# Two graph-attention layers on one core: programs written out, first row factors spread by TensorE, layer 0 results in three pieces, head parts moved among the groups

## The chip, the core and the metric

The kernel runs on one core of one Trainium2 chip. The metric is the device time of one execution in microseconds (us). The engines are TensorE (PE, with its weight loads as PEld), VectorE (DVE), ScalarE (ACT), GpSimd (POOL) and SyncE (SP), each with a queue of instructions of its own that it works off in order; they wait for one another by semaphores.

## The reference

Eight graphs of 2048 nodes with 256 features, a dense adjacency matrix each, two attention layers with a residual:

```python
h = relu(layernorm(x));  x = x + gnn0(h, adj)      # one head
h = relu(layernorm(x));  x = x + gnn1(h, adj)      # four heads of 64 columns
# gnn: f = h W^T (+ b);  s_src, s_dst = f a_src, f a_dst
#      e[i, j] = leaky_relu(s_src[i] + s_dst[j], 0.2), masked where adj[i, j] == 0
#      out[i] = softmax_j(e[i, :]) f
```

A row without any edge gives the mean of f.

## The kernel before

**Factors instead of a softmax over pairs.** exp(leaky_relu(s + d)) is a product of a factor of the row and one of the column, with two different pairs of factors, for s + d above and below zero. Layer 0 makes tiles max(row factor, column factor) * mask (DVE, line 1214, `A` events) and multiplies them with the weighted features (PE, line 1006). Layer 1 compares row and column factors (ACT, line 782, or for a few groups DVE, line 1258), masks the bits for "negative" (DVE, line 1278, `N`) and "positive" (DVE, line 1282, `S`), and multiplies those bits as fp8 with features that are split into three bf16 parts (`Sw`) and two fp16 parts (`Sv`) (PE, lines 1022 and 1028, `G` events; a group is four column blocks of one head). The row factors of a chunk have to lie along the free axis on all 128 partitions, in `Rb`: five rows, one for layer 0 and four for the heads. Before, they are transposed (PE, line 944), moved (ACT, line 683), written to `R_dram` and read back with a broadcast (SP, lines 379 and 384).

**Chunks, batches, steps.** A graph (batch) has 4 chunks of 512 rows. Layer 1 runs five chunks behind layer 0 (`B_LAG`), so for each batch b = 1 to 7 there are these steps:

- the **first step** (`slot_f`): layer 0 of chunk 0 (16 `A` tiles on PE) beside the last features of layer 1 of batch b - 1: `T1` and `F1` are the transposes and products of a half chunk, `MV` moves a product out, `Y1` and `N1` are ACT's moves and normalisations for them. Then the maxima (`MX`, DVE `MAX` and `SHIFT`), exponentials (ACT `exps`), the mean (`MN`, `MEANL`), the rows (`RW`), and the parts of heads 0 and 1: `W` weighs them (DVE, line 1130), `first_part` rounds (ACT, line 697), `LF` takes off the first part (DVE, line 1135), `second_part` (ACT, line 701), `LS` gives the third (DVE, line 1140); POOL weighs and subtracts for `Sv` (lines 489 and 494), ACT rounds (lines 708, 713).
- **AB1**, **AB2**, **AB3**: layer 0 of chunks 1 to 3 beside layer 1 of the batch before; 16 `A` tiles and 16 `G` groups. AB1 also makes the parts of heads 2 and 3. After the last group of a head ACT moves the sums out (lines 809 to 812, `EB`) and POOL finishes the head (lines 553 to 574). After the last tile ACT moves the sums of layer 0 out (line 740, `EA`) and DVE adds them to x and takes the statistics for the next layernorm (`X1`: lines 1231 to 1246, then 1062 and 1066).
- the **last step** (`slot_g`): layer 1 of the last chunk beside the features of layer 0 of the next batch (`T`, `FE`).

**What sets the order.** The lists of events that `order`, `slot_f` and `slot_g` write by hand; each engine picks its own events out of them. `vector_order` puts an `A` tile between `N` and `S` where one stands ahead of a group. ACT compares up to `LEAD` groups ahead, into two slots (`CRING`); the tiles of layer 0 have four slots (`RING`). PE, DVE and ACT run batches 1 to 6 in a hardware loop (`looped`, line 314), batch 0 and batch 7 written out; SP and POOL are written out throughout.

## Time and profile before

| | |
|---|---|
| median of 3 runs | 2997.63 us (2993.99 to 3000.18) |
| the profiled execution | 2994.71 us, of it the span 2992.9 us |
| granted TensorE clock, mean | 0.952 of full |
| busy: PE, DVE, ACT, POOL | 85%, 66%, 55%, 46% of the span |

A row of the timeline gives start, duration, engine, line, operation, what it writes and reads, how many instructions are merged (x), and in brackets the idle time of the engine before it and what ended that. A fp32 product stands in the trace as two MATMUL rows' worth of count, so an `A` tile is x8. The table of stretches gives each engine's busy time, then the granted clock and the DMA share. The steps of a batch end where ACT moves the sums of layer 0 out (line 740): in the second batch at 649.9, 735.8, 811.8, 886.1 and (the next first step) 1011.5 us.

### The profile page before, as it was taken

How to read it: one execution, taken by the hardware profiler on the slowest of the kernel's cores; microseconds unless marked ns; L12 is line 12 of the kernel's file. 1: busy time of each engine (PE TensorE's matmuls, PEld its weight loads, DVE VectorE, ACT ScalarE, POOL GpSimd, SP SyncE). 2: the span in 40 equal slices, each digit the busy share in tenths (PEclk: the TensorE clock that was granted, in tenths of full speed). 3: DMA queues.
4: the chain of work that ended last, by engine and by line, in shares of the span. 5: the costliest groups of instructions: out<-in, count | busy, mean ns of one | idle time of the engine just before them, and what ended most of it. 6: DMA issues, size and time to landing. Idle time of an engine off the chain costs nothing.

```text
span 2992.9 us, 60549 instructions
## 1 busy us (share of the span) xinstructions
PE 2530.4 (85%) x22166; PEld 2261.4 (76%) x22166; DVE 1966.6 (66%) x3342; ACT 1660.0 (55%) x3170; POOL 1370.9 (46%) x1757
## 2 busy tenths in 40 slices
PE   4988799878998799987999879988799888996686
PEld 3876688867887588875888768887688867886676
DVE  1544666766666676657667576665666676668996
ACT  4124655645567465655556465664655655554664
POOL 2111445534455354443455434454444444446566
PEclk9998899989999899998999989999899999999899
DMA  7682244242442444422443324423244242211120
GB/s 131 70 96 38 36 75 72 45 80 40 71 74 51 68 62 74 72 48 48 75 76 62 57 41 75 75 54 65 36 74 76 52 75 35 62 36 36 37 54 19
DMA packets 332958, 181.38 MB, mean 61 GB/s; under 512 B 278240, under 2 KB 279392, under 8 KB 332640
## 3 DMA queue, kind: packets, MB, share of 16 engines
q1 hardware_dynamic: 314208, 143.64, 22.0%
q0 software_dynamic: 18432, 33.56, 13.0%
q8 instruction: 192, 3.15, 0.4%
q14 instruction: 126, 1.03, 0.1%
HBM read 193.60 MB, written 50.66 MB: 82 GB/s over the span
## 4 chain that ended last, share of the span: by engine, by line
PE 54%; DVE 19%; ACT 14%; issue 9%; POOL 3%; DMA 0%; DVEq 0%; ACTq 0%; SPq 0%; POOLq 0%
PE accA L1006 24%; PE accB L1022 12%; PE accB L1028 8%; ACT shared L782 8%; DVE shared L1258 4%; PE misc_ps L914 4%; DVE shared L1214 3%; DVE shared L1278 3%; PE accA L889 3%; ACT shared L621 2%; DVE xb L1239 1%; DVE xb L1246 1%; DVE stats L1062 1%; PE misc_ps L904 1%; PE accA L878 1%
## 5 line engine op out<-in xcount | busy, mean ns | idle before, releaser
L782 ACT ACTIVATE shared<-Rb,dd 128x512 int8<-128x512 f32 x1616 | 1017.7, 718 | 382.2 <-DVE shared L1278 381.9
L1006 PE MATMUL accA<-S,shared 128*128 128x257 f32 x4096 | 1009.3, 400 | 179.1 <-DVE shared L1214 162.2
L1022 PE MATMUL accB<-Sw,shared 128*128 128x195 bf16 x7680 | 978.5, 250 | 85.8 <-DVE shared L1282 56.5
L1006 PEld LDWEIGHTS accA<-S,shared 128*128 128x128 f32 x4096 | 794.7, 199 | 322.7 <-DVE shared L1214 195.9
L1028 PE MATMUL accB<-Sv,shared 128*128 128x130 f16 x7680 | 763.9, 223 | 0.0
L1022 PEld LDWEIGHTS accB<-Sw,shared 128*128 128x128 fp8e4 x7680 | 642.2, 99 | 142.3 <-issue 103.8
L1214 DVE SCALAR_TENSOR_TENSOR shared<-Rb,dd,mask 128x512 f32<-128x512 f32 x512 | 457.3, 909 | 268.1 <-PE accA L1006 213.9
L1028 PEld LDWEIGHTS accB<-Sv,shared 128*128 128x128 fp8e4 x7680 | 577.9, 99 | 0.9
L553 POOL TENSOR_SCALAR shared<-shared 128x260 f32<-128x260 f32 x128 | 136.9, 1070 | 761.8 <-ACT shared L812 719.7
L1278 DVE TENSOR_TENSOR shared<-shared,mask 128x512 uint32<-128x512 uint32 x512 | 402.1, 785 | 125.6 <-ACT shared L782 118.6
L1282 DVE TENSOR_TENSOR shared<-shared,mask 128x512 uint32<-128x512 uint32 x512 | 413.5, 808 | 12.0
L1258 DVE TENSOR_SCALAR shared<-Rb,dd 128x512 uint8<-128x512 f32 x432 | 245.3, 631 | 13.0 <-PE accB L1028 13.0
L809 ACT ACTIVATE shared<-accB 128x390 f32<-128x390 f32 x120 | 58.7, 489 | 319.2 <-PE accB L1028 283.8
L1079 DVE TENSOR_TENSOR S<-misc_ps,bias 128x264 f32<-128x264 f32 x128 | 54.7, 427 | 223.1 <-PE misc_ps L914 222.7
L914 PE MATMUL misc_ps<-WT,yT 128*128 128x264 f32 x512 | 147.5, 412 | 55.4 <-ACT yT L650 54.2
L494 POOL TENSOR_TENSOR S<-S,Sv 128x1040 f32<-128x1040 f32 x32 | 70.5, 2203 | 199.3 <-ACT Sv L708 199.3
L567 POOL TENSOR_TENSOR denB<-denB,minus_one 128x4 f32<-128x4 f32 x128 | 149.7, 1169 | 23.5 <-POOL denB L565 23.5
L914 PEld LDWEIGHTS misc_ps<-WT,yT 128*128 128x128 f32 x512 | 93.4, 199 | 72.6 <-ACT yT L650 58.7
L889 PE MATMUL accA<-WT,shared 128*128 128x258 f32 x512 | 125.8, 393 | 21.2 <-ACT S L658 21.2
L740 ACT ACTIVATE shared<-accA 128x1028 f32<-128x1028 f32 x32 | 32.9, 1027 | 189.8 <-PE accA L1006 189.8
L474 POOL TENSOR_SCALAR var_eps<-mv 128x4 f32<-128x4 f32 x64 | 23.8, 372 | 228.3 <-DVE mv L1066 226.2
L889 PEld LDWEIGHTS accA<-WT,shared 128*128 128x128 f32 x512 | 95.0, 194 | 41.9 <-ACT S L658 29.6
(106 smaller groups left out, 2566.1 us busy)
## 6 DMA issues: line engine op xcount, KB each, us to landing
Rb<-R_dram SPq DMA_DIRECT2D x160, 256.0 KB, 3.6
adj_bytes<-in_adj POOLq DMA_DIRECT2D x128, 256.0 KB, 5.3
xb<-in_x SPq DMA_DIRECT2D x32, 512.0 KB, 5.0
out<-xb SPq DMA_DIRECT2D x32, 512.0 KB, 3.6
mask<-adj_bytes SPq DMA_TRANSPOSE x256, 4.1
shared<-in_W SPq DMA_DIRECT2D x2, 256.0 KB, 3.1
R_dram<-R_rows SPq DMA_DIRECT2D x8, 32.0 KB, 1.8
shared<-in_a SPq DMA_DIRECT2D x8, 0.2 KB, 10.6
```

The lines of the kernel that those rows point to most:

```text
L553: pool.tensor_scalar(low, low, 1 / LOW, None, ALU.mult)
L567: pool.tensor_tensor(denB[:, :], denB[:, :], minus_one[:, :], ALU.pow)\
L782: last = nc.scalar.activation(cmp[:, slot, jj // 2, of_pair(jj % 2, 0, CI)], Rb[:, h, :], ACT.Sign, bias=w[1][:, JG * g + jj, h:h + 1], sc ...
L889: last = nc.tensor.matmul(accA[:, 2 + k % 2, 0:E0], yT[:, t % 2, kc, k * P:(k + 1) * P], WT[0][:, kc, :], start=kc == 0, stop=kc == KC - 1)
L914: last = nc.tensor.matmul(misc_ps[:, 0:E1], yT1[:, kc, k * P:(k + 1) * P], WT[1][:, kc, :], start=kc == 0, stop=kc == KC - 1)
L1006: last = nc.tensor.matmul(accA[:, k, 0:F + 1], tiles[:, j % RING, k * P:(k + 1) * P], S0[:, j, 0:F + 1], start=j == 0, stop=j == NJ - 1)
L1022: nc.tensor.matmul(acc[:, bank, col:col + NS], bits[:, g % BRING, 1, jj // 2, of_pair(jj % 2, k * P, P)], Sw[:, j, h, :, :].rearrange("p a ...
L1028: last = nc.tensor.matmul(acc[:, bank, col:col + NN], bits[:, g % BRING, 0, jj // 2, of_pair(jj % 2, k * P, P)], Sv[:, j, h, :, :].rearran ...
L1214: nc.vector.scalar_tensor_tensor(out=tiles[:, j % RING, :], in0=Rb[:, H, :], scalar=w[0][:, j, :], in1=mask[:, n % 2, j // 2, of_pair(j % ...
L1258: last = nc.vector.tensor_scalar(bits_u8[:, g % BRING, 0, jj // 2, of_pair(jj % 2, 0, CI)], Rb[:, h, :], w[1][:, JG * g + jj, h:h + 1], 25 ...
L1278: nc.vector.tensor_tensor(n_bits, src.bitcast(u32), chunk_mask, ALU.bitwise_and)\
L1282: nc.vector.tensor_tensor(s_bits, n_bits, chunk_mask, ALU.bitwise_xor)\
```

## The change

Four things, all in the order of work and in how the first chunk's rows come about; the arithmetic of the outputs is unchanged.

1. PE, DVE and ACT have no hardware loop any more: all eight batches are written out.
2. For chunk 0 the row factors no longer go through DRAM: `spread_rows` on PE (event `SP`) transposes each factor column, broadcast to 128 columns, into PSUM (4 transposes for layer 0, 16 for layer 1, into `accB` and `misc_ps`), and `move_first_rb` on ACT copies them to `Rb` (1 or 4 copies of 128x512). SP loads `Rb` only for chunks 1 to 3. `turn_rows` waits until the copies are made.
3. `X1` is cut into `X1` (sum of the mean), `X2` (sum of layer 0), `X3` (statistics), which stand among the first groups of the next step; the last half product of a chunk is moved out there too (`("MV", 7)`), and `T1`, `F1` stand later in the steps.
4. In AB1 the first group stands ahead of the first tiles, two groups are compared at the start, and the parts of heads 2 and 3 are spread over the first four groups. In the first step all four `F1` and one `T1` stand between the tiles, and `MX`, `MN`, `RW` two or three tiles later.

```diff
-    def order(do_a, do_b, do_l, stats=None, x1_before=False, parts=False, feats=False):
+
+    def order(do_a, do_b, do_l, stats=None, first=False, feats=False, results=(), late_move=False):
         events = []
+        x1, x2, x3 = [[(x, 1)] * bool(results) for x in ("X1", "X2", "X3")]
         for h in range(H):
             last = h == H - 1
             a = [[("A", G * h + i)] * do_a for i in range(G)]
             g = [[("G", h, i)] * do_b for i in range(G)]
             load = [("L", 2, h)] * do_l
-            early = [("X1", 1)] * (x1_before and h == (0 if do_b else 1))
             st = [("ST", stats)] * (stats is not None and h == (2 if do_b else H - 1))
             eb = [("EB", h)] * do_b
             if last:
-                events += a[0] + [("MV", 1)] * feats + a[1] + a[2] + a[3] + [("EA",)] * do_a + g[0] + [("F1", 3)] * feats
-                events += g[1] + [("MV", 2)] * feats + load + g[2] + g[3] + st * (not do_b)
-                events += [("X1", 0)] * (do_a and do_b) + [("MV", 3)] * feats + eb
-            elif h == 0 and parts:
-                events += a[0] + a[1] + [("NM", 2), ("W", 2), ("HI", 2)] + g[0] + [("LF", 2), ("MID", 2), ("HIGH", 2)]
-                events += g[1] + [("NR", 2), ("LS", 2)] + a[2] + [("NM", 3), ("W", 3), ("HI", 3)] + load + g[2]
-                events += [("LF", 3), ("MID", 3), ("HIGH", 3), ("LOW", 2)] + a[3]
-                events += g[3] + [("NR", 3), ("LS", 3)] + early + eb + [("LOW", 3)]
+                events += a[0] + [("MV", 1)] * feats + a[1] + [("F1", 2)] * feats + a[2] + a[3] + [("EA",)] * do_a
+                events += g[0] + g[1] + load + g[2] + [("MV", 2), ("F1", 3)] * feats + g[3] + st * (not do_b)
+                events += [("X1", 0)] * ("end" in results) + [("MV", 3)] * (feats and not do_b) + eb
+            elif h == 0 and first:
+                events += g[0] + a[0] + a[1] + [("NM", 2), ("W", 2), ("HI", 2)] + g[1] + [("LF", 2), ("MID", 2), ("HIGH", 2)]
+                events += a[2] + [("NR", 2), ("LS", 2), ("NM", 3), ("W", 3), ("HI", 3)] + load + g[2] + [("LOW", 2)]
+                events += a[3] + [("LF", 3), ("MID", 3), ("HIGH", 3)] + x1 + g[3] + [("NR", 3), ("LS", 3)] + eb
+                events += [("LOW", 3)]
+            elif h == 0:
+                events += a[0] + a[1] + [("MV", 7)] * late_move + g[0] + x1 + g[1] + x2 + a[2] + load + g[2] + x3
+                events += a[3] + g[3] + eb
             else:
                 on1, on2 = feats and h == 1, feats and h == 2
-                events += early * (not do_b) + [("N1", 0)] * on1 + a[0] + a[1] + g[0] + [("F1", 1)] * on2 + g[1]
-                events += [("T1", 0), ("Y1", 0), ("N1", 1)] * on1 + [("MV", 0)] * on2 + a[2] + load + g[2]
-                events += [("F1", 0)] * on1 + [("T1", 1), ("Y1", 1)] * on2 + a[3] + st + g[3] + [("F1", 2)] * on2
-                events += early * do_b + eb
+                t0 = [("T1", 0), ("Y1", 0), ("N1", 1)] * on1
+                f0 = [("F1", 0)] * on1
+                late = x2 * (first and h == 1), x3 * (first and h == 1)
+                events += [("N1", 0)] * (on1 and not first) + a[0] + late[0] + a[1] + g[0] + late[1] + [("F1", 1)] * on2
+                events += [("N1", 0)] * (on1 and first) + g[1] + (not first) * t0 + [("MV", 0)] * on2
+                events += a[2] + load + g[2] + (first * t0 or f0) + a[3] + st
+                events += [("T1", 1), ("Y1", 1)] * on2 + g[3] + first * f0 + eb
...
-    STEP_AB = [None] + [order(1, 1, 1, stats=1, x1_before=c == 1, parts=c == 1, feats=True) for c in range(1, NC)]
-    STEP_AB_LAST = [None] + [order(1, 1, c < NC - 2, x1_before=c == 1, parts=c == 1, feats=True)
-                             for c in range(1, NC)]
+    STEP_AB, STEP_AB_LAST = [[None] + [order(1, 1, more or c < NC - 2, stats=1 if more else None, first=c == 1, feats=True,
+                                             results=["before"] + ["end"] * (c == NC - 1), late_move=c > 1)
+                                       for c in range(1, NC)] for more in (True, False)]
...
-        def looped(eng, prog):
-            start(prog)
-            with eng.Fori(1, B - 1) as b:
                 batch(prog, b, True)
             end(prog)
...
             def features(b, L=0):
                 store_rows(b, L)
-                for u in [H] if L == 0 else range(H):
-                    load_rb(b, 0, u)
...
+            def move_first_rb(b, L):
+
+                act.wait_ge(S["misc_done"], 4 * layer_index(b, L) + 3)
+                for u in [H] if L == 0 else range(H):
+                    src = misc_ps[:, :] if u >= H - 1 else accB[:, u, :]
+                    nc.scalar.activation(Rb[:, u, :], src, ACT.Copy).then_inc(S[f"rb_made{L}"], 1)
...
             def slot_f(b, beside):
+                move_half(b - 1, NC - 1, 0)
+                norm_half(b - 1, NC - 1, 1)
+                if beside:
+                    scale_features(2)
                 move_half(b - 1, NC - 1, 1)
                 if beside:
-                    for t in range(2, NC):
-                        scale_features(t)
+                    scale_features(3)
                 exps(b - 1, 1)
+                move_first_rb(b - 1, 1)
                 first_part(b - 1, 0)
                 move_rows(b - 1, 1)
...
-                ahead, nxt = {}, mine[0] + 1
+                ahead, nxt = {}, mine[1 if kind == "AB1" else 0] + 1
                 for e in events:
                     if e[0] == "G":
                         i = G * e[1] + e[2]
-                        upto = min(i + (LEAD - 1 if i < G else LEAD), HG - 1)
+                        upto = min(i + (LEAD if i >= G else LEAD - 2 if kind == "AB1" else LEAD - 1), HG - 1)
...
-            looped(act, Program(features, lambda: None, step, slot_f, slot_g))
+            written_out(Program(features, lambda: None, step, slot_f, slot_g))
...
-            def turn_rows(b, L):
+            def spread_rows(b, L):
                 i = layer_index(b, L)
                 pe.wait_ge(S["exp_ready"], 2 * i + 2)
                 pe.wait_ge(S["misc_used"], 3 * i + 2)
+                if L == 1:
+                    pe.wait_ge(S["b_moved"], H * NC * b + 1)
+                for u in [H] if L == 0 else range(H):
+                    dst = misc_ps if u >= H - 1 else accB[:, u, :]
+                    for k in range(CH):
+                        last = nc.tensor.transpose(dst[:, k * P:(k + 1) * P], R[:, u, k:k + 1].to_broadcast([P, P]),
+                                                   ident[:, :])
+                last.then_inc(S["misc_done"], 1)
+
+            def turn_rows(b, L):
+                i = layer_index(b, L)
+                pe.wait_ge(S[f"rb_made{L}"], (b + 1) * (1 if L == 0 else H))
...
-                events = [("A", 0), ("F1", 2), ("A", 1), ("F1", 3), ("A", 2), ("A", 3), ("MX",), ("A", 4), ("A", 5), ("MN",),
-                          ("A", 6), ("RW",)] + [("A", j) for j in range(7, NJ)]
+                events = [("F1", 0), ("A", 0), ("F1", 1), ("A", 1), ("T1", 1), ("A", 2), ("F1", 2), ("A", 3), ("F1", 3),
+                          ("A", 4), ("A", 5), ("MX",), ("A", 6), ("A", 7), ("MN",), ("A", 8), ("SP",), ("A", 9),
+                          ("RW",)] + [("A", j) for j in range(10, NJ)]
...
-                          ("G", 2, 1), ("FE", 3), ("G", 2, 2), ("MX",), ("G", 2, 3), ("MN",), ("G", 3, 0), ("RW",),
-                          ("G", 3, 1), ("T1", 0), ("G", 3, 2), ("F1", 0), ("G", 3, 3), ("F1", 1), ("T1", 1)]
+                          ("G", 2, 1), ("FE", 3), ("G", 2, 2), ("MX",), ("G", 2, 3), ("MN",), ("G", 3, 0), ("SP",),
+                          ("G", 3, 1), ("RW",), ("G", 3, 2), ("T1", 0), ("G", 3, 3)]
...
-                events = [("A", 0), ("A", 1), ("A", 2), ("MV", 2), ("A", 3), ("MV", 3), ("MAX",), ("A", 4), ("A", 5),
-                          ("SHIFT",), ("W", 0), ("A", 6), ("MEANL",), ("A", 7), ("LF", 0), ("A", 8), ("A", 9), ("LS", 0), ("A", 10),
-                          ("W", 1), ("A", 11), ("A", 12), ("LF", 1), ("A", 13), ("LS", 1), ("A", 14), ("A", 15)]
+                events = [("A", 0), ("A", 1), ("MV", 0), ("A", 2), ("MV", 1), ("A", 3), ("MV", 2), ("A", 4), ("MV", 3), ("MAX",),
+                          ("A", 5), ("A", 6), ("SHIFT",), ("W", 0), ("A", 7), ("MEANL",), ("A", 8), ("LF", 0), ("A", 9),
+                          ("A", 10), ("LS", 0), ("W", 1), ("A", 11), ("A", 12), ("LF", 1), ("A", 13), ("A", 14), ("LS", 1),
+                          ("A", 15)]
...
+                    events += {("G", 0, 0): [("X2", 1), ("MV", 7)], ("G", 0, 1): [("X3", 1)]}.get(e, [])
...
                         last.then_inc(S["a_sum"], 1)
+                        continue
+                    if e[0] == "X2":
+                        n1 = n - e[1]
+                        xs = xb[:, n1 % XSLOTS, :, :]
                         dve.wait_ge(S["a_rec"], n1 + 1)
...
                         last.then_inc(S["x1_ready"], 1)
+                        continue
+                    if e[0] == "X3":
+                        n1 = n - e[1]
                         dve.wait_ge(S["x1_ready"], n1 + 2)
```

Where the instructions moved, as they stand in the built programs. First DVE in the middle of the first step (batch 7 of before, batch 1 of the change; all four rows with `Rb` are tiles of layer 0, `split` and `Sw` are the head parts), before:

```order
L1106 TENSOR_SCALAR ss<-ss 128x64
L1110 MEMSET S 128x64
L1130 TENSOR_TENSOR split<-S,wv 128x1040
L1214 SCALAR_TENSOR_TENSOR shared<-Rb,dd,mask 128x512
L1119 SCALAR_TENSOR_TENSOR mean_h<-misc_ps,bias 128x264
L1214 SCALAR_TENSOR_TENSOR shared<-Rb,dd,mask 128x512
L1135 TENSOR_TENSOR split<-split,Sw 128x1040
L1214 SCALAR_TENSOR_TENSOR shared<-Rb,dd,mask 128x512 x2
L1140 TENSOR_TENSOR Sw<-split,Sw 128x16x65
```

and of the change:

```order
L1139 TENSOR_SCALAR ss<-ss 128x64
L1143 MEMSET S 128x64
L1163 TENSOR_TENSOR split<-S,wv 128x1040
L1249 SCALAR_TENSOR_TENSOR shared<-Rb,dd,mask 128x512
L1152 SCALAR_TENSOR_TENSOR mean_h<-misc_ps,bias 128x264
L1249 SCALAR_TENSOR_TENSOR shared<-Rb,dd,mask 128x512
L1168 TENSOR_TENSOR split<-split,Sw 128x1040
L1249 SCALAR_TENSOR_TENSOR shared<-Rb,dd,mask 128x512 x2
L1173 TENSOR_TENSOR Sw<-split,Sw 128x16x65
```

The sequence is the same, but it stands one tile later in the step: the single tiles are `A` 6 and 7 before, and `A` 7 and 8 now.

Then ACT at the same place, before:

```order
L672 ACTIVATE R<-ss 128x16x4
L676 ACTIVATE dd<-dd 128x64
L697 ACTIVATE Sw<-split 128x16x65
L683 ACTIVATE R_rows<-misc_ps 128x128
L701 ACTIVATE Sw<-split 128x16x65
```

and of the change:

```order
L678 ACTIVATE R<-ss 128x16x4
L682 ACTIVATE dd<-dd 128x64
L690 ACTIVATE Rb<-accB 128x512 x3
L690 ACTIVATE Rb<-misc_ps 128x512
L710 ACTIVATE Sw<-split 128x16x65
L696 ACTIVATE R_rows<-misc_ps 128x128
L714 ACTIVATE Sw<-split 128x16x65
```

The copies of the spread rows stand between the exponentials and the first rounding of head 0.

Last DVE from the end of AB1 into AB2 (before: batch 7):

```order
L1282 TENSOR_TENSOR shared<-shared,mask 128x512
L1231 TENSOR_SCALAR alone_now<-shared 128x4
L1232 TENSOR_SCALAR alone<-shared 128x4
L1233 TENSOR_SCALAR denA<-shared 128x4
L1236 RECIPROCAL denA<-denA 128x4
L1239 SCALAR_TENSOR_TENSOR xb<-mean_h,alone_now,xb 128x256 x4
L1246 SCALAR_TENSOR_TENSOR xb<-shared,denA,xb 128x256 x4
L1062 BN_STATS stats<-xb 128x6 x4
L1066 BN_AGGR mv<-stats 128x2 x4
L1079 TENSOR_TENSOR S<-misc_ps,bias 128x264
L1214 SCALAR_TENSOR_TENSOR shared<-Rb,dd,mask 128x512 x2
L1258 TENSOR_SCALAR shared<-Rb,dd 128x512 x4
```

and of the change:

```order
L1324 TENSOR_TENSOR shared<-shared,mask 128x512
L1249 SCALAR_TENSOR_TENSOR shared<-Rb,dd,mask 128x512 x2
L1112 TENSOR_TENSOR S<-misc_ps,bias 128x264
L1300 TENSOR_SCALAR shared<-Rb,dd 128x512 x4
L1320 TENSOR_TENSOR shared<-shared,mask 128x512
L1324 TENSOR_TENSOR shared<-shared,mask 128x512
L1266 TENSOR_SCALAR alone_now<-shared 128x4
L1267 TENSOR_SCALAR alone<-shared 128x4
L1268 TENSOR_SCALAR denA<-shared 128x4
L1271 RECIPROCAL denA<-denA 128x4
L1274 SCALAR_TENSOR_TENSOR xb<-mean_h,alone_now,xb 128x256 x4
L1300 TENSOR_SCALAR shared<-Rb,dd 128x512 x4
```

The result of the chunk moved from ahead of the first group's comparison to behind it; line 1079 (now 1112) is the move of the last half product.

## Rows read from the trace of the kernel before

**Rows 1.** The page, parts 1 and 4: busy time by engine; the chain that ended last.
```profile
PE 2530.4 (85%) x22166; PEld 2261.4 (76%) x22166; DVE 1966.6 (66%) x3342; ACT 1660.0 (55%) x3170; POOL 1370.9 (46%) x1757
...
PE 54%; DVE 19%; ACT 14%; issue 9%; POOL 3%; DMA 0%; DVEq 0%; ACTq 0%; SPq 0%; POOLq 0%
```

**Rows 2.** Stretches: AB1, AB2, AB3, last plus first step looped, the same written out.
```profile
649.90:735.80 85.90, 65.79 (x535) 58.06 (x536) 55.92 (x88) 55.68 (x94) 34.41 (x41) 0.90 0.23 38
735.80:811.80 76.00, 71.23 (x667) 65.68 (x666) 50.66 (x92) 44.51 (x82) 37.09 (x53) 0.98 0.44 74
811.80:886.10 74.30, 69.44 (x666) 64.06 (x664) 50.75 (x92) 44.43 (x81) 37.15 (x53) 1.00 0.43 72
886.10:1011.50 125.40, 108.06 (x908) 93.56 (x905) 83.57 (x140) 65.67 (x146) 61.52 (x74) 0.96 0.36 67
2333.50:2451.30 117.80, 105.27 (x907) 92.02 (x904) 83.67 (x140) 65.65 (x146) 62.00 (x74) 0.99 0.38 65
```

**Rows 3.** Timeline at the loop's edge, second to third batch: all engines.
```profile
968.08 2.88 DVE L1214 SCALAR_TENSOR_TENSOR shared<-Rb,dd,mask 128x512 f32<-128x512 f32 x3 [3.15 <-issue]
...
969.01 1.07 PE L1006 MATMUL accA<-S,shared 128*128 128x257 f32 x2 [3.29 <-DVE shared L1214]
```

**Rows 4.** Timeline at the same place of batch 7, written out: PE.
```profile
2413.14 2.00 PE L1006 MATMUL accA<-S,shared 128*128 128x257 f32 x8
```

**Rows 5.** Timeline of a first step from the maxima on: PE, DVE, ACT.
```profile
620.58 0.60 PE L926 MATMUL misc_ps<-ident,d_part 128*128 128x128 f32 x4
...
623.38 1.24 DVE L1130 TENSOR_TENSOR split<-S,wv 128x1040 f32<-128x1040 f32 x1 [0.64 <-ACT dd L676]
...
624.54 0.78 DVE L1214 SCALAR_TENSOR_TENSOR shared<-Rb,dd,mask 128x512 f32<-128x512 f32 x1
624.66 1.09 ACT L697 ACTIVATE Sw<-split 128x1040 bf16<-128x1040 f32 x1 [1.31 <-DVE split L1130]
...
625.58 0.43 DVE L1119 SCALAR_TENSOR_TENSOR mean_h<-misc_ps,bias 128x264 f32<-128x264 f32 x1 [0.26 <-PE misc_ps L936]
...
627.62 1.23 DVE L1135 TENSOR_TENSOR split<-split,Sw 128x1040 f32<-128x1040 f32 x1
```

**Rows 6.** Timeline: nearest rows to a spread and to its copies.
```profile
240.77 1.09 PE L904 MATMUL misc_ps<-ident,y 128*128 128x128 f32 x4 [3.65 <-ACT y L639]
...
730.74 0.60 ACT L812 ACTIVATE shared<-accB 128x520 f32<-128x520 f32 x1
```

**Rows 7.** Timeline of the end of a first step and of AB1.
```profile
649.92 1.03 ACT L740 ACTIVATE shared<-accA 128x1028 f32<-128x1028 f32 x1 [5.04 <-PE accA L1006]
...
651.23 3.73 PE L1006 MATMUL accA<-S,shared 128*128 128x257 f32 x16 [1.43 <-ACT shared L740]
...
654.24 0.69 DVE L1282 TENSOR_TENSOR shared<-shared,mask 128x512 uint32<-128x512 uint32 x1
...
663.83 2.19 POOL L494 TENSOR_TENSOR S<-S,Sv 128x1040 f32<-128x1040 f32 x1 [10.34 <-ACT Sv L708]
663.87 2.69 DVE L1214 SCALAR_TENSOR_TENSOR shared<-Rb,dd,mask 128x512 f32<-128x512 f32 x1
...
666.62 3.80 PE L1006 MATMUL accA<-S,shared 128*128 128x257 f32 x8 [5.68 <-DVE shared L1214]
...
687.27 2.94 PE L1006 MATMUL accA<-S,shared 128*128 128x257 f32 x6 [8.54 <-DVE shared L1214]
```

**Rows 8.** Timeline of AB1's last move and of AB2's opening.
```profile
727.69 1.16 PE L914 MATMUL misc_ps<-WT,yT 128*128 128x264 f32 x4 [2.48 <-ACT yT L650]
...
736.88 0.17 DVE L1231 TENSOR_SCALAR alone_now<-shared 128x4 f32<-128x4 f32 x1 [4.91 <-ACT shared L740]
...
737.52 2.49 DVE L1239 SCALAR_TENSOR_TENSOR xb<-mean_h,alone_now,xb 128x256 f32 x4
...
748.58 3.33 DVE L1258 TENSOR_SCALAR shared<-Rb,dd 128x512 uint8<-128x512 f32 x4
...
753.92 0.62 PE L1022 MATMUL accB<-Sw,shared 128*128 128x195 bf16 x4 [2.29 <-DVE shared L1282]
```

More of the change, by code:

```diff
@@ L523, in slot_g @@
                 at = STEP_B.index(("EB", 1))
[L524 removed]
+                step("G", [("X3", 1)] + STEP_B[:at] + [("ST", 1)] * more + STEP_B[at:], b, NC)
             def step(kind, events, b, c):
@@ L796, in step @@
                     compare(mine[0])
+                if kind == "AB1":
+                    compare(mine[1])
                 for e in events:
```

65 lines of the change are left out of this document (34 added, 31 removed), and 4 rows, old and new, of the table events.

## The prediction, made before the changed kernel ran

> **What bounds the kernel now.** I read the page first: TensorE is busy 85% of the span and holds 54% of the chain that ended last, VectorE 19% of it [rows 1]. That makes every idle stretch of PE the thing to look for. The table of stretches then shows where they are [rows 2]: AB2 and AB3 have 71.2 and 69.4 us of PE work in 76.0 and 74.3 us and are bound by PE. AB1 has less work (65.8) and takes 85.9 us, and its granted clock is 0.90, so TensorE also ran there at 1.2 instead of 2.4 GHz for a fifth of the time. Last and first step together take 125.4 us in the loop, but 117.8 us for the same work in batch 7, which is written out. The timeline says what PE waits for: DVE, whose queue is in order and is itself held by ACT and POOL.
>
> From these rows two prices that I use below: a tile of layer 0 costs PE 3.73 / 2 = 1.87 us [rows 7], and a group 2.3 us (AB2's 71.2 less 16 tiles, four half products of 1.16 [rows 8] and two transposes of half tiles, over 16).
>
> **The change, part by part.** Sums are per batch, and stand against the profiled execution's own 2994.7 us; the median of the runs shown is 2.9 us above that, so I add to 2997.6.
>
> *Loops written out.* At the loop's edge DVE starts 3.15 us late without any wait for another engine, and PE's first tile comes after 3.29 us of idle time [rows 3]; in batch 7 the first tile has no idle time before it and its x8 take 2.00 us [rows 4]. The whole difference is 125.4 - 117.8 = 7.6 us, and there are five such edges (the last one leaves the loop and is the 117.8 itself): **-38 us**.
>
> *The first step.* This is where I expect to lose. Its parts, against the written-out 117.8:
> - Its first instruction on PE is now the half product `F1` 0, which waits for ACT's move `Y1` 0. That stands on ACT behind the move of the last head's sums (three operations, the longest 0.60, [rows 6]), which waits for the last group. So PE idles about 2.7 us where it idled 0.6 before: +2.1, and +1.0 for the slower clock after it.
> - The spread for layer 0: 4 transposes, +0.6. For layer 1: 16 transposes. I take 4 x 0.5 = 2.0 us at 2.4 GHz, from the x4 that took 0.60 with its latency [rows 5]. The row at 1.2 GHz has 1.09 for four [rows 6], so 4.4 us is the other end.
> - `MX` moved behind tile 5, but DVE still has only one tile made ahead of it. From the end of `MX` (621.18) to the end of the tile behind the weighing `W` 0 (625.32) are 4.1 us [rows 5], and PE now has one tile (1.87) to cover them, where it had two: +2.3. The next tile stands directly behind the mean, which PE makes just ahead of it: 0.43 + 0.78 less 0.3 of today: +1.0.
> - The largest: on ACT the four copies of the spread rows stand ahead of the first rounding (line 697, now 710), they wait for the spread, the spread stands on PE behind tile 8, and DVE takes tile 9 only after `LF` 0, which waits for that rounding. So tile 8, spread, copies, rounding, `LF` 0 and tile 9 are one chain. Four copies of 512 columns at 0.5 each (0.60 for 520 columns [rows 6], less the 0.1 by which one overlaps the next), 1.09, 1.23 and 0.78 [rows 5] make 5.1 us in which PE has nothing. +5.1.
> - `RW` now follows tile 9 and ACT's second rounding waits for it, as do `LS` 0, `W` 1 and tile 11; with the slower clock after 5 us of idle time: +2.0.
>
> Together **+16 us** for each of batches 2 to 7. For batch 1 the half products that are spread among tiles now stood alone ahead of the tiles before, with waits like the 3.65 us at 240.77 [rows 6], so only +8. In all +104. Bounds: +6 a batch if DVE finds its rounding ready (only real work and the opening are left), +20 if the spread runs at 1.2 GHz.
> The trip through DRAM that is removed hid behind other work here: no comparison waits for a row transfer of chunk 0. It was bare only at the start of the program (-4), and at its end the copies lengthen the chain to the first group (+2.5).
>
> *AB1.* Before, PE idles 1.43, 5.68 and 8.54 us [rows 7] and three times under 1.1: 17.6 us in all until the second group of head 1. The 5.68 is a tile behind `LS` 2, which waits for ACT; the 8.54 is tile 4 behind the whole result `X1`. Both orders are mended. But the first group is now first on PE, and its bits need the move of the sums, a comparison, `N` and `S`: from 649.92 to 654.93 [rows 7], so PE idles 5.3 us there instead of 1.43. I followed DVE's new queue with the durations of rows 5 and 7. Four POOL operations of 2.2 us fall into this step, and each holds a DVE operation that meets it until it ends (a tile took 2.69 instead of 0.78 beside one, [rows 5, 7]). Then the third group's bits come 2.2 us late, the fourth's 3.3, tile 5 0.8, the second group of head 1 1.7: with the opening 13.3 us. That is -4.3. The late move `Y1` 1 ahead of `F1` 2 (2.48 us, [rows 8]) goes, since a group and two tiles now cover it: -2.5. Fewer waits raise the clock from 0.90, tile rows of 3.80 against 2.00 us being its price [rows 4, 7]: -2.2. **-9 a batch**, -63 in all; between -4 (more operations held) and -15 (none).
>
> *AB2 and AB3.* They too lose the 2.48: -2.5 each. But their opening gets worse. The second group waits for bits that DVE compares itself, 2.29 us now [rows 8]. In the change, DVE's queue there begins with the move of the last half product, which comes at the same distance from the last group. From it to the second group's bits, two tiles (1.5) leave and the result's first part enters (four small ones of about 0.17, then 2.49): +1.7. The tile behind it waits for `X2` on top, about 1.3, where the clock was full before. So -0.8 for AB2, +0.5 for AB3: **-2 us** for seven batches. Bounds for the two together: -5 to +6 a batch, since a comparison of four rows took 3.33 us [rows 8] beside POOL's work and may take half of that without it.
>
> *The last step* gets 0.4 us longer (a transpose behind the second group waits for ACT's later normalisation): +3.
>
> Sum: -38 + 104 - 4 + 2.5 - 63 - 2 + 3 = +2.5, so **3000 us**.
>
> **The rivals.**
> 1. *Faster.* The held operations of DVE fall into its own waits. In AB1 DVE waits for ACT twice in this stretch, and if three of the four 1.9 us fall there, AB1 gains 6 more: -42, 2958. For it speaks that DVE is busy for only 56 of AB1's 86 us [rows 2]; against it that today three of four do hit an operation that PE waits for.
> 2. *Slower.* The result's pieces make DVE the bound at 14 openings. `X1`, `X2` and `X3` are 8 us of DVE work that stood where DVE waited 4.91 us for the sums [rows 8], and now stand where PE has no bits in store. If POOL's last head slows them as it slowed 2.49 and 3.33, each opening costs 3 us more: +42, 3042. It decides from the point at which DVE's work between the last half product and the second group's bits exceeds what PE has to do there, a group, two tiles and a group (8.3 us). Against it: 1.7 and 1.3 of it are counted above.
> 3. *Slower.* The spread of layer 1 runs at 1.2 GHz and leaves the clock there for the tile behind it: four transposes took 1.09 us in such a stretch [rows 6] against 0.60 [rows 5], so 4.4 us instead of 2.0, and a tile 3.80 [rows 7] against 2.00 [rows 4]: +4 a batch, +28, 3028. The row at 0.60 stood in a stretch of full clock and speaks against it; the idle time ahead of tile 7 speaks for it. The Trainium skill ("TensorE: Matmul & The Clock Gate", "Part 4: PE-mode transpose") has the full clock not engaging for transposes, which do not count as PE-busy in the same way; that is this rival. No stretch of before has so many transposes in a row, so no row here decides it.
> 4. *The change doesn't do what it says.* Written-out code may have to be fetched while it runs, and the 7.6 us may come back as pauses spread over the batch: 3038. Batch 7 speaks against it. The Trainium skill ("Runtime: NRT & Kernel Launch", "Instruction fetch mechanics") does too: sequential code is fetched ahead, and a taken branch outside the window stalls; the 3.15 us of rows 3 agree, and by it the sum stays.
>
> **How the numbers follow.** A measurement of this kernel can tell 0.2% (6 us) from no change. My own case, gains and losses cancel: 0.36, alone 2980 to 3020 (of it faster 0.08, same 0.17, slower 0.11). Rival 1: 0.32, faster. Rival 2: 0.18, rival 3: 0.08, rival 4: 0.06, slower. That is 0.40 faster, 0.17 same, 0.43 slower. The range takes in the bounds of AB1 and the first step as far as 8 in 10: 2955 to 3045.
>
> **What would show it.** Right: no pause without a releaser on DVE between batches; in every first step PE idle about 5 us ahead of tile 9, released by a DVE tile, and DVE idle for ACT's line 710; AB1 near 77 us; last plus first step near 134 us; AB2 and AB3 near 75. Wrong: last plus first step under 125 us (then the chain through the copies is not bare, and I am too high by up to 60), AB1 over 82, or AB2 and AB3 over 78 (rival 2).

## The result, and the profile of the changed kernel

The changed kernel takes 3040.6 us (median; 3039.6 to 3046.0), the kernel before 2996.0 beside it: a ratio of 1.015, with a 95% interval of 1.013 to 1.017. It is slower by 45 us, where I forecast 3000. The profiled execution has a span of 3038.2 us against 2992.9 before.

Parts 1 and 4 of the changed kernel's page, which answer to [rows 1]:

```profile
PE 2563.2 (84%) x22326; PEld 2305.3 (76%) x22326; DVE 1951.3 (64%) x3342; ACT 1686.2 (55%) x3210; POOL 1395.4 (46%) x1757
...
PE 58%; DVE 17%; ACT 14%; issue 7%; POOL 4%; SPq 0%; DMA 0%; POOLq 0%; ACTq 0%; DVEq 0%
```

Read alone, they tell almost nothing: PE has 160 matmuls more and nearly the same share of the span. The stretches say more. This is the table by stretch of batch 3, to be held against [rows 2]: AB1, AB2, AB3, last plus first step (from one evacuation of layer 0's sums to the next; then PE, PEld, DVE, ACT and POOL busy, the granted clock, the DMA share and GB/s).

```profile
1030.10:1112.40 82.30, 66.54 (x535) 59.60 (x535) 60.11 (x91) 56.23 (x94) 33.07 (x38) 0.90 0.27 47
1112.40:1186.40 74.00, 71.01 (x666) 65.61 (x665) 50.45 (x93) 44.59 (x81) 39.13 (x53) 0.98 0.42 76
1186.40:1260.20 73.80, 69.65 (x667) 64.29 (x666) 49.15 (x91) 44.62 (x82) 38.05 (x53) 1.00 0.41 73
1260.20:1395.40 135.20, 109.64 (x927) 96.63 (x924) 78.95 (x138) 68.14 (x151) 63.29 (x77) 0.96 0.28 47
```

AB1 went from 85.9 to 82.3 us (I expected 77), AB2 from 76.0 to 74.0 and AB3 from 74.3 to 73.8 (expected 75), last plus first step from 125.4 to 135.2 (expected 134). The other batches repeat the four within 0.2 us, but for batch 1: 81.2 for AB1, 74.1 for AB3, and 137.1 for its last step with the next first step. Batch 1's own first step grew from 84.4 to 98.5, the part behind the last evacuation from 303.6 to 317.1.

The pause of DVE without a releaser at the loop's edge, 3.15 us in [rows 3], is gone. In its place DVE now waits for an engine, the half product `F1` 0:

```profile
967.49 1.40 DVE L1249 SCALAR_TENSOR_TENSOR shared<-Rb,dd,mask 128x512 f32<-128x512 f32 x2
976.50 0.43 DVE L1112 TENSOR_TENSOR S<-misc_ps,bias 128x264 f32<-128x264 f32 x1 [7.61 <-PE misc_ps L934]
```

In the timeline the first step looks as forecast. Changed kernel, first step of batch 3, PE; rows with a wait and the spread between them:

```profile
975.30 1.16 PE L934 MATMUL misc_ps<-WT,yT 128*128 128x264 f32 x4 [2.20 <-ACT yT L656]
...
994.78 3.13 PE L1039 MATMUL accA<-S,shared 128*128 128x257 f32 x8 [2.54 <-DVE shared L1249]
...
1000.54 2.00 PE L1039 MATMUL accA<-S,shared 128*128 128x257 f32 x8 [1.19 <-DVE shared L1249]
1002.38 1.47 PE L969 MATMUL accB<-ident,R 128*128 128x128 f32 x12
1003.69 0.60 PE L969 MATMUL misc_ps<-ident,R 128*128 128x128 f32 x4
1009.42 3.54 PE L1039 MATMUL accA<-S,shared 128*128 128x257 f32 x8 [5.13 <-DVE shared L1249]
...
1019.51 4.69 PE L1039 MATMUL accA<-S,shared 128*128 128x257 f32 x13 [4.71 <-DVE shared L1249]
```

These are the waits of `F1` 0, of tile 7, of the tile behind the mean, of tile 9, and one that I had not priced by itself, 4.71 us at tile 11. ScalarE and VectorE show why tile 9 is late. ACT first, then DVE:

```profile
1004.39 1.58 ACT L690 ACTIVATE Rb<-accB 128x512 f32<-128x512 f32 x3 [11.71 <-PE misc_ps L969]
1005.84 0.62 ACT L690 ACTIVATE Rb<-misc_ps 128x512 f32<-128x512 f32 x1
1006.31 1.11 ACT L710 ACTIVATE Sw<-split 128x1040 bf16<-128x1040 f32 x1
...
1007.46 1.24 DVE L1168 TENSOR_TENSOR split<-split,Sw 128x1040 f32<-128x1040 f32 x1 [6.97 <-ACT Sw L710]
1008.62 1.41 DVE L1249 SCALAR_TENSOR_TENSOR shared<-Rb,dd,mask 128x512 f32<-128x512 f32 x2
```

The rounding (line 710) needs only 1.1 us, but DVE has been idle for it for 6.97 us: it stands behind four copies, which wait for the spread.

What I had not seen is in AB1. Its openings are there (5.26, 3.01, 1.36, 0.36, 1.47 us; I had worked out 13.3 together, they are 11.5), and then comes a wait that my list lacks. Changed kernel, AB1 of batch 3, POOL, DVE, ACT and PE:

```profile
1064.43 0.87 POOL L559 TENSOR_SCALAR shared<-shared 128x260 f32<-128x260 f32 x1 [7.59 <-DVE xb L1257]
...
1065.69 0.38 DVE L1099 BATCH_NORM_AGGREGATE mv<-stats 128x2 f32<-128x6 f32 x4
...
1073.41 0.91 POOL L580 TENSOR_TENSOR xb<-xb,shared 128x256 f32<-128x256 f32 x1 [0.18 <-POOL shared L576]
1074.41 0.56 POOL L480 TENSOR_SCALAR var_eps<-mv 128x4 f32<-128x4 f32 x1
...
1077.12 0.20 POOL L487 TENSOR_TENSOR shift<-rstd,neg_mean 128x4 f32<-128x4 f32 x1
...
1077.43 1.09 ACT L645 ACTIVATE y<-xb,shift,rstd 128x256 f32<-128x256 f32 x2 [5.72 <-issue]
...
1078.67 1.09 PE L924 MATMUL misc_ps<-ident,y 128*128 128x128 f32 x4 [4.31 <-ACT y L645]
1079.55 3.63 PE L1039 MATMUL accA<-S,shared 128*128 128x257 f32 x8
```

PE waits for `T1` 0, that for ACT's normalisation `N1` 0 (line 645), that for POOL's `shift` (line 487). DVE has the statistics ready at 1066.07 (line 1099), but POOL works on head 0's sums (lines 559 to 580, the event `EB` 0) until 1074.3, since `X3` comes behind `EB` 0 in its queue. The profile calls the wait of ACT "issue" and names no engine; the releaser had to be found by following what the instruction reads.

### The profile page after: what moved, and what is told of

It reads as the page before. It is cut to its first block, busy times and chain, and to the rows that moved or that the text cites. A ratio compares the mean times of both kernels' runs of the same rounds, so it can differ in the third digit from the quotient of the medians.

```text
span 3038.2 us, 57409 instructions
## 1 busy us (share of the span) xinstructions
PE 2563.2 (84%) x22326; PEld 2305.3 (76%) x22326; DVE 1951.3 (64%) x3342; ACT 1686.2 (55%) x3210; POOL 1395.4 (46%) x1757
## 4 chain that ended last, share of the span: by engine, by line
PE 58%; DVE 17%; ACT 14%; issue 7%; POOL 4%; SPq 0%; DMA 0%; POOLq 0%; ACTq 0%; DVEq 0%
PE accA L1039 25%; PE accB L1055 13%; PE accB L1061 9%; ACT shared L798 6%; PE misc_ps L934 4%; DVE shared L1300 4%; PE accA L909 3%; DVE shared L1320 2%; ACT shared L627 2%; DVE xb L1274 2%; DVE shared L1249 1%; DVE shared L1324 1%; DVE split L1163 1%; PE misc_ps L924 1%; DVE xb L1285 1%
## 5 line engine op out<-in xcount | busy, mean ns | idle before, releaser
L1055 PE MATMUL accB<-Sw,shared 128*128 128x195 bf16 x7680 | 993.2, 253 | 159.0 <-DVE shared L1324 95.5
L1055 PEld LDWEIGHTS accB<-Sw,shared 128*128 128x128 fp8e4 x7680 | 651.1, 100 | 213.1 <-issue 177.6
L1061 PE MATMUL accB<-Sv,shared 128*128 128x130 f16 x7680 | 775.2, 225 | 0.0
L1061 PEld LDWEIGHTS accB<-Sv,shared 128*128 128x128 fp8e4 x7680 | 588.2, 100 | 2.1
L1249 DVE SCALAR_TENSOR_TENSOR shared<-Rb,dd,mask 128x512 f32<-128x512 f32 x512 | 426.0, 846 | 203.6 <-PE accA L1039 200.6
L1320 DVE TENSOR_TENSOR shared<-shared,mask 128x512 uint32<-128x512 uint32 x512 | 395.9, 773 | 138.8 <-ACT shared L798 128.7
L1324 DVE TENSOR_TENSOR shared<-shared,mask 128x512 uint32<-128x512 uint32 x512 | 442.1, 863 | 12.2
L1300 DVE TENSOR_SCALAR shared<-Rb,dd 128x512 uint8<-128x512 f32 x432 | 227.0, 589 | 14.2 <-PE accB L1061 14.2
L934 PEld LDWEIGHTS misc_ps<-WT,yT 128*128 128x128 f32 x512 | 94.0, 195 | 33.6 <-ACT yT L656 19.3
L569 POOL TENSOR_TENSOR shared<-shared 128x260 f32<-128x260 f32 x128 | 101.1, 790 | 23.5 <-POOL shared L566 23.5
L495 POOL TENSOR_TENSOR S<-S,v 128x1040 f32<-128x1040 f32 x32 | 68.9, 2153 | 92.9 <-DVE split L1163 88.5
```

Of the source, the lines that this page charges most:

```text
L934: last = nc.tensor.matmul(misc_ps[:, 0:E1], yT1[:, kc, k * P:(k + 1) * P], WT[1][:, kc, :], start=kc == 0, stop=kc == KC - 1)
L1055: nc.tensor.matmul(acc[:, bank, col:col + NS], bits[:, g % BRING, 1, jj // 2, of_pair(jj % 2, k * P, P)], Sw[:, j, h, :, :].rearrange("p a ...
L1061: last = nc.tensor.matmul(acc[:, bank, col:col + NN], bits[:, g % BRING, 0, jj // 2, of_pair(jj % 2, k * P, P)], Sv[:, j, h, :, :].rearran ...
L1249: nc.vector.scalar_tensor_tensor(out=tiles[:, j % RING, :], in0=Rb[:, H, :], scalar=w[0][:, j, :], in1=mask[:, n % 2, j // 2, of_pair(j % ...
L1300: last = nc.vector.tensor_scalar(bits_u8[:, g % BRING, 0, jj // 2, of_pair(jj % 2, 0, CI)], Rb[:, h, :], w[1][:, JG * g + jj, h:h + 1], 25 ...
L1320: nc.vector.tensor_tensor(n_bits, src.bitcast(u32), chunk_mask, ALU.bitwise_and)\
```

## Experiments

Ten kernels. Times are medians, each beside the kernel before, which had 2990 to 2994 in these runs. Run names are those of the headings.

### e1_loops_out: the loops alone

```diff
-            looped(pe, Program(features, lambda: None, step, slot_f, slot_g))
+            written_out(Program(features, lambda: None, step, slot_f, slot_g))
```
(in the kernel before; the same for `act` and `dve`)

> The kernel before with the loops of TensorE, VectorE and ScalarE written out, nothing else. My theory (the term 'loops written out', -38): the five edges of 7.6 us go, so about 2958 us (2950 to 2966), with all six stretches of last and first step at 117 to 119 us instead of five at 125.4, and no pause of VectorE without a releaser between batches. Rival (the written-out code is fetched while it runs, rival 4): the edges' time comes back as pauses without a releaser elsewhere; 2990 us or more.

Measured: 2956.5 us against 2993.6, ratio 0.988 (0.986 to 0.989), so -37.1. The six stretches of last and first step take 115.8 to 117.9 us, where [rows 2]'s written-out line has 117.8 and the looped one 125.4:

```profile
1229.30:1346.60 117.30, 104.82 (x907) 92.10 (x904) 81.68 (x138) 65.62 (x145) 62.65 (x74) 0.99 0.36 67
```

The term of -38 stands, and rival 4 is out. By the stretches the five edges gave 42 us and the first batch's, which I had not counted, 3 more (84.4 to 81.3); AB1 to AB3 and the ends took some 7 of them back. Most of that is AB3, 75.7 us instead of 74.3 at a granted clock of 0.98 instead of 1.00. The waits without a releaser ahead of DVE's tiles (line 1214) went from 19.3 us in five waits to 0.2 us, and ACT's ahead of line 650, 11.5 us in five, are gone.

### e3_norm_first: POOL's order in AB1

The changed kernel, in POOL's step:

```diff
+                if kind == "AB1":
+                    events = [e for e in events if e != ("X3", 1)]
+                    at = events.index(("EB", 0))
+                    events = events[:at] + [("X3", 1)] + events[at:]
```

> The changed kernel (3040.6 us), but in the first combined step GpSimd does the normalization that ScalarE's first move-over waits for ahead of the eight operations on head 0's sums, and no longer behind them. Theory: the idle of TensorE of 4.28 us ahead of the first transposition (line 924) of this step hangs on these eight operations; moved, it falls to under 1 us, that step falls from 82.3 to about 78.5, and the time by seven of these, to about 3012 us (3008 to 3020). Rival: head 0's sums come 3 us later and the wait turns up behind them (ScalarE's copies of the sums of head 1, then TensorE at head 2's first group): the step stays within 1 us of 82.3 and the time at 3035 or more. Second rival: another late work (transposed tiles, a comparison) stands right behind; about half of the gain, 3025.

Measured: 2992.6 us, ratio to the kernel before 0.9999 (0.999 to 1.001). Four small operations, moved past ten others (I had counted eight) on an engine that is busy for 33 of 82 us, give -48 (-45 by the ratios), about as much as the changed kernel loses in all. AB1 is 75.1 in every batch. POOL and ACT in AB1 now:

```profile
1052.16 0.47 POOL L480 TENSOR_SCALAR var_eps<-mv 128x4 f32<-128x4 f32 x1 [9.43 <-DVE mv L1103]
...
1054.85 0.34 POOL L487 TENSOR_TENSOR shift<-rstd,neg_mean 128x4 f32<-128x4 f32 x1
1055.16 0.87 POOL L563 TENSOR_SCALAR shared<-shared 128x260 f32<-128x260 f32 x1
...
1057.49 1.08 ACT L649 ACTIVATE y<-xb,shift,rstd 128x256 f32<-128x256 f32 x2
...
1064.02 0.69 POOL L584 TENSOR_TENSOR xb<-xb,shared 128x256 f32<-128x256 f32 x1 [0.18 <-POOL shared L580]
```

The gain is 7.1 a batch where the idle was 4.3, so my 28 us were low by 20. Most of the rest is the clock, and the stretch shows it:

```profile
1016.00:1091.20 75.20, 64.06 (x536) 57.69 (x536) 60.05 (x91) 55.95 (x95) 33.14 (x38) 0.93 0.32 51
```

PE does the same matmuls in 64.06 us and no longer in 66.54, at 0.93 instead of 0.90. In the changed kernel PE starts again behind the wait at 0.50 (the lower level, 1.2 GHz), as the rows in the last section show. Both rivals fall: head 0's sums come 4.5 us later in the step and nobody waits for them.

### e4_steps_only and e5_steps_norm: the steps' new order without the new first step

e4: the kernel before, written out, with the change's `order`, its result in three pieces, the comparisons further ahead and the B steps' order; first step, the last step's tail and all rows through DRAM as before. e5 is e4 with the four lines of e3_norm_first. The pieces that differ from the changed kernel, in TensorE's program:

```diff
-                events = [("F1", 0), ("A", 0), ("F1", 1), ("A", 1), ("T1", 1), ("A", 2), ("F1", 2), ("A", 3), ("F1", 3),
-                          ("A", 4), ("A", 5), ("MX",), ("A", 6), ("A", 7), ("MN",), ("A", 8), ("SP",), ("A", 9),
-                          ("RW",)] + [("A", j) for j in range(10, NJ)]
+                events = [("A", 0), ("F1", 2), ("A", 1), ("F1", 3), ("A", 2), ("A", 3), ("MX",), ("A", 4), ("A", 5), ("MN",),
+                          ("A", 6), ("RW",)] + [("A", j) for j in range(7, NJ)]
```

> The kernel before, written out, with the new order of the steps AB1, AB2, AB3 and of the matching parts of the B steps (layer 0's results in three pieces, the parts of heads 2 and 3 among the groups, comparisons further ahead), but the first step of a batch, the tail of the last one and the rows through DRAM as before. Theory: AB1 82.3 and AB2, AB3 74.0 and 73.7 as in the changed kernel, last and first step at 118: 2958 less 27 less 18 is 2913, and some 8 us more in the end part from the first B step: 2915 to 2925. Rival: what AB1 and the others gain in the changed kernel is only work handed to the first step (the F1 0, F1 1, T1 1 moves), so the last and first step grow by as much here: 2945 to 2960.

> As the run before it (new order of AB1 to AB3 and B, first step and rows of before), with GpSimd's normalization ahead of the operations on head 0's sums in AB1. Theory: AB1 near 78.5, so 4 us a batch less, 2885 to 2897. Rival (the wait turns up behind head 0's sums, which come 3 us later): no difference to the run before it, within 5 us.

Measured: e4 2910.6 us, ratio 0.972 (0.970 to 0.974); e5 **2865.9 us**, ratio 0.957 (0.956 to 0.959). e4 against e1 is -45.9, so the new order of the steps is a gain of its own and no loan from the first step: last plus first step stays at 118.1 to 119.4. e5 against e4 is -44.7: the same wait, worth the same as in the changed kernel. Both came out under my ranges. For e4 I had put 8 us on the end part, which grew by 1.2. For e5 I had again priced the wait at its length alone, and it is 19 us under the range. e5 beats both kernels, by 4.3% and 5.7%. Its stretches, AB1 and last plus first step:

```profile
971.40:1046.50 75.10, 61.88 (x535) 55.72 (x536) 59.97 (x91) 55.90 (x94) 33.03 (x38) 0.98 0.32 49
...
1194.70:1312.70 118.00, 104.83 (x907) 91.99 (x904) 80.68 (x138) 65.72 (x145) 62.92 (x77) 0.99 0.37 67
```

AB1 has the same length as in e3 although its clock is 0.98 instead of 0.93 and PE is busy for 2.2 us less: once the wait is gone, AB1 waits for DVE's bits, and what a faster PE saves in work it idles at its five openings, 13.1 us in e5 and 11.0 in e3.

### e2_part_first: the rounding ahead of the copies

The changed kernel, ScalarE, first step:

```diff
-                move_first_rb(b - 1, 1)
                 first_part(b - 1, 0)
+                move_first_rb(b - 1, 1)
```

> The changed kernel (3040.6 us) with one swap in ScalarE's program of the first step: head 0's first part (line 710) goes ahead of the four copies of the spread rows, and no longer behind them. Theory (the chain tile 8, spread, four copies, rounding, LF 0, tile 9 of my prediction costs 5.1 us a batch): TensorE's 5.12 us ahead of tile 9 nearly go, seven times, and the time falls by 30 to 40 us, to about 3005; the last and first step goes from 135.2 to about 130. Rival: the second rounding (line 714) still stands behind the rows' copy, and VectorE's LS 0 and tile 11 take the time back: under 10 us saved, 3030 or more.

Measured: 3010.0 us, ratio 1.006 (1.005 to 1.008), so 31 us less than the changed kernel (26 by the ratios to the kernel before). Last plus first step is 130.2 to 132.9. PE in the first step of the next batch:

```profile
1352.51 2.00 PE L1039 MATMUL accA<-S,shared 128*128 128x257 f32 x8 [1.18 <-DVE shared L1249]
1358.41 0.33 PE L976 MATMUL misc_ps<-ident,R 128*128 128x128 f32 x1 [0.42 <-ACT Rb L690]
...
1365.19 10.16 PE L1039 MATMUL accA<-S,shared 128*128 128x257 f32 x38 [4.72 <-DVE shared L1249]
```

The 5.13 at tile 9 is gone and the 4.7 at tile 11 stayed: the chain through the copies is real, and its idle time has the size that I gave it. The stretch got only 2.3 to 5.0 us shorter, because the clock takes part of the gain back. Where it is 132.9 the waits are the same as in these rows, but tile 7 and tiles 11 to 15 ran partly at 0.50: 3.42 and 11.50 us instead of 2.00 and 10.59 (all 40 rows).

### e6_rows_dram and e9_rows0_spread: layer 1's rows back through DRAM

e6 is the changed kernel with these edits (and the counts of `misc_done` that go with them); e9 is e6 with the four lines of e3_norm_first.

```diff
             def features(b, L=0):
                 store_rows(b, L)
+                for u in range(H) if L == 1 else []:
+                    load_rb(b, 0, u)
...
-                move_first_rb(b - 1, 1)
...
-                        spread_rows(fb, fl)
+                        if fl == 0:
+                            spread_rows(fb, fl)
```

> The changed kernel with layer 1's first chunk of rows through DRAM as before (no spread and no ScalarE copies in the first step, layer 0's spread kept), everything else as changed. Theory (spread, copies and the waits behind them are 9.7 us a batch of the first step by my terms 0.6 + 2.0 + 5.1 + 2.0): last and first step from 135.2 to about 125.5, first B work no later, and the time about 60 to 70 us lower, near 2975. Rival 1: the moved order (F1, maxima and rounding two tiles later) is what costs, and the spread lies in its shadow: 3020 or more. Rival 2: the trip through DRAM then arrives late for AB1, whose compares come earlier now: AB1 grows by over 2 us a batch.

> The changed kernel with GpSimd's normalization first in AB1 (as e3_norm_first) and layer 1's rows through DRAM (as e6_rows_dram): what is left of the change against e8_order_only (2918.3 us) is the spread of layer 0's row alone. Theory: e6_rows_dram less the 45 to 48 us of the normalization, 2935 to 2938, so layer 0's spread, ScalarE's copy and the rows' copy behind it cost about 18 us or 3 to 4 us a batch in the last step (129.5 against 125.5). Rival: the two undoings share their gain (the same low clock), and the time is 2950 or more.

Measured: e6 2982.6 us, ratio 0.9975 (0.9965 to 0.9986), 58 us under the changed kernel (53 by the ratios); e9 2939.5 us, ratio 0.982 (0.981 to 0.984). Last plus first step is 129.3 to 129.7 in e6 (127.4 once), where I expected 125.5, so I had the spread 4 us a batch too dear there: it takes 5.7 us of it, and 9.1 in the first batch's first step. AB1 did not grow, so the trip through DRAM arrives in time. e9 is 1.5 us over my range. It lies 43 under e6 and 53 under e3, and its last plus first step at 128.8 stands 3.3 above e8's, which follows.

### e7_spread_only, e8_order_only, e10_spread_swap: one half at a time, on e5

e7 is e5 with layer 1's rows spread, in the first step's order of before (`("A", 6), ("SP",), ("A", 7), ("RW",)`); e8 is e5 with the change's order of the first step and of the last one's tail, rows through DRAM; e10 is e7 with the swap of e2_part_first.

> The kernel of the run e5_steps_norm (2865.9 us) with layer 1's first chunk of rows spread by TensorE and copied by ScalarE, in the first step's order of before. Theory: as the undoing of it, 9 to 10 us a batch, 2926 to 2936, with last and first step at 127 to 128. Rival: with tiles, maxima and rounding in the order of before the chain has two tiles of slack and the spread costs only its own 2.6 us: 2880 to 2890.

> The kernel of the run e5_steps_norm (2865.9 us) with the changed kernel's order of the first step and of the last one's tail (F1 0, F1 1, T1 1 and VectorE's moves in the first step, maxima and mean two tiles later), rows through DRAM. Theory: F1 0's wait 2.1, the wait ahead of tile 7 of 2.3, ahead of the tile behind the mean 1.0, and the clock, 6 to 8 us a batch: 2910 to 2925. Rival: the order costs as much as the whole of last and first step's 17 us and the spread nothing: 2980 or more. Third possibility: the order alone is worth nothing either way (2866), and it costs only together with the spread.

> The kernel of e7_spread_only (2912.2 us; layer 1's row spread, order of before) with head 0's first part ahead of the four copies. Theory: of the 46 us that the spread costs there, TensorE's idle of 2.58 us ahead of tile 8 hangs on the copies in ScalarE's queue (7 x 2.6 = 18), and the rest is the spread's own time on TensorE: 2890 to 2897, still above e5_steps_norm (2865.9). Rival: the copies are needed as early by the rows' transposition, whose wait then shows instead: 2905 or more.

Measured: e7 2912.2 (ratio 0.974, 0.972 to 0.975), e8 2918.3 (0.975, 0.974 to 0.977), e10 2889.8 (0.966, 0.964 to 0.968). So on e5 the order alone costs 52, the spread alone 46. e7 lies between my theory and the rival: its row on PE in the first step is

```profile
1316.88 1.35 PE L1055 MATMUL accA<-S,shared 128*128 128x257 f32 x5 [2.58 <-DVE shared L1264]
```

2.58 us bare instead of 5.13. From the end of the spread (1311.75) to this tile it is 5.13 us here too, but the spread stands behind tile 6, and tile 7 (1.90 us) is made ahead of `LF` 0 and lies ready behind it. e10 takes these away and is 22 us faster, as expected; 24 us remain over e5: the 16 transposes (1.9 us, seven times, and 3.7 once at the end) and what is left of the waits. In neither order of ScalarE does the spread pay for a DMA round trip that nobody waited for.

In e8 the wait at tile 11 shows alone. e5 has none there; its longest one behind `RW` stands ahead of tile 14. PE of e8, then of e5, and DVE of e8:

```profile
1326.18 4.22 PE L1018 MATMUL accA<-S,shared 128*128 128x257 f32 x9 [4.71 <-DVE shared L1225]
```
```profile
1308.97 3.30 PE L1019 MATMUL accA<-S,shared 128*128 128x257 f32 x14 [2.32 <-DVE shared L1228]
```
```profile
1322.31 3.11 DVE L1142 TENSOR_TENSOR split<-S,wv 128x1040 f32<-128x1040 f32 x1
```

`LS` 0 and `W` 1 now stand back to back ahead of tile 11 on DVE, and `W` 1 took 3.11 us there beside POOL's work, against 1.24 alone [rows 5]. In e5 a tile stands between the two and takes the hold (2.67 us), and PE's waits behind `RW` are four, 3.6 us together. So this place gives only 1.1 of the 7.4 us by which the order lengthens the stretch. 3.7 come from the waits of tiles 7 and 8, 2.54 and 1.18 us, which e5 does not have; 1.2 are more busy time of PE at 0.96 of the clock instead of 0.99, and most of the rest is the wait of `F1` 0, 2.19 us.

### The ladder

Each line differs from the one above it in one thing.

| kernel | us | step |
|---|---|---|
| before | 2993.6 | |
| e1: loops written out | 2956.5 | -37.1 |
| e4: + new order of AB1 to AB3 and B | 2910.6 | -45.9 |
| e5: + normalisation ahead of `EB` 0 | 2865.9 | -44.7 |
| e8: + new order of first step and tail | 2918.3 | +52.4 |
| e9: + layer 0's row spread | 2939.5 | +21.2 |
| e3: + layer 1's rows spread | 2992.6 | +53.1 |
| changed kernel: normalisation behind `EB` 0 | 3040.6 | +48.0 |

The runs of one kernel lay within 1 to 10 us of each other. By the ratios to the kernel before, which had 2990.2 to 2996.0 us beside these kernels, every step comes out within 2.6 us of the one given. So a step is good to about 3 us.

## Why the prediction was right or wrong

The time came out 40.6 us above the forecast, near the upper end of the range (3045) and outside my own case's 2980 to 3020. None of the four rivals is what happened. That the range holds the time is in part luck: it was made wide for AB1's openings and the first step, and not for the wait that made the difference.

*Loops written out*, -38: right, -37.1.

*The first step*, *the last step*, *start and end*: 104 + 3 - 4 + 2.5 = +105.5 against 52.4 + 21.2 + 53.1 = +126.7. The shape was right: near 134 for last plus first step, and 135.2 measured. Within it, the waits of `F1` 0 (2.20; I had 2.7), tile 7 (2.54; 2.3) and the tile behind the mean (1.19; 1.0) came as worked out. The chain through the copies (5.1) came as 5.13, and e2 takes 31 us away with it; e7 adds that with the spread one tile earlier only 2.6 of it is bare. Two sizes were off. The batch that I discounted (+8 for batch 1) paid in full: its first step is 98.5 against 81.3 in e1, +17. And the end, priced at the chain to the first group (+2.5), grew from 304.9 in e1 to 317.1: the same first step stands there once more with no tiles to hide it. Together the two are 19 us over my terms, nearly the 21 that are missing. (On e5, whose end part is 304.8, the order alone makes it 312.1 and the spread alone 309.4.)

*AB1*, -9 a batch: this is the step that failed, since the term left out a wait. It measured -3.6. What I listed came better than I had it: 85.9 to 75.1 in e3 and e5, -10.8 a batch or -75 against my -63. But a wait was missing from the list. I followed DVE's new queue and ScalarE's, and took POOL only as the engine that slows DVE. The change put `X3` behind `EB` 0 in POOL's queue, and I counted neither what is queued ahead of the normalisation there (ten operations, 9.9 us) nor who waits for it (`N1` 0, then `T1` 0, then everything on PE). Price: 48 us by e3, 44.7 by e5. The mark "AB1 over 82" was hit by 82.3.

*AB2 and AB3*, -2: mis-sized, -2.0 and -0.6 a batch in the changed kernel, -18 in all. The late move ahead of `F1` 2 went as predicted (no PE wait there now; 2.48 before [rows 8]), but the opening cost less:

```profile
1131.22 0.50 PE L1055 MATMUL accB<-Sw,shared 128*128 128x195 bf16 x4 [2.99 <-DVE shared L1324]
```

2.99 against 2.29 [rows 8], +0.7 and not +1.7 at 14 openings, and the tile behind it waits for `X2` in AB3 alone (1.15 us; I had 1.3). Rival 2 was this term with the opposite sign, and 74.0 against its mark of 78 removes it.

*Rival 1* (POOL-held operations fall into DVE's waits) did not come: four operations of DVE in AB1 beside POOL's work still took 2.33 to 3.13 us, and the openings gained 1.8 us on my 13.3, not 6. *Rival 3* (the spread at 1.2 GHz) fell for the seven spreads that stand between tiles. In the first table are the stretch of the 16 transposes of batch 3, the idle time behind it, and tile 9:

```profile
1001.90:1004.30 2.40, 2.39 (x19) 2.01 (x18) 0.00 (x0) 0.00 (x0) 0.00 (x0) 1.00 0.00 0
1004.30:1009.10 4.80, 0.00 (x0) 0.00 (x0) 1.64 (x2) 3.04 (x5) 0.00 (x0) 1.00 0.01 2
1009.20:1012.50 3.30, 3.08 (x7) 2.51 (x8) 0.82 (x2) 0.00 (x0) 0.00 (x0) 0.50 0.00 0
```

The transposes ran at 1.00 of the clock, from 1002.38 to 1004.29, 1.9 us, as did the other six. So 2.0 was right there. The eighth spread, in the end part, is the one that rival 3 describes: it ran at 0.50 and took 3.64 us, where I had 4.4 as the other end. Its stretch, and the one behind it:

```profile
2800.40:2804.10 3.70, 3.64 (x16) 3.27 (x16) 0.00 (x0) 0.00 (x0) 1.96 (x1) 0.50 0.00 0
2804.60:2807.90 3.30, 0.33 (x1) 0.14 (x1) 0.64 (x1) 2.79 (x6) 0.00 (x0) 1.00 0.00 0
```

The Trainium skill ("TensorE: Matmul & The Clock Gate", "Part 4: PE-mode transpose") has the full clock not engaging for transposes. This trace does not bear that out. Seven spreads ran at full speed, though there the tiles ahead of them had it already. At the end the clock had been at 0.50 for 20 us and stood at 1.00 from 2804.6 on, right behind 3.64 us in which PE did nothing but transposes.

*Rival 4* fell with e1. The Trainium skill ("Runtime: NRT & Kernel Launch", "Instruction fetch mechanics") has sequential code fetched ahead and a taken branch outside the window stall. The trace agrees as far as it goes: without the loops DVE's waits without a releaser fell from 19.3 us to 0.2, and no such pauses came up on DVE or ACT in their place; PE's are 18.6 us in all where they were 15.3. That the edge was a matter of fetching, and not of other work that a loop brings, no run here shows.

The sum missed by 40 because a wait that isn't on the list has no bounds. Without it (e3) the kernel takes 2992.6 us, 7 from the forecast, but that nearness is luck: AB1, AB2 and AB3 came out 28 us better than their terms, the first steps and the ends 21 us worse, and the two cancel.
